# A feed-forward with ternary weights: four f32 passes become four f16 products with x1 split in two

## What is computed

```python
def _L0_ffn_ref(x, weight, bias):
    scale = jnp.mean(jnp.abs(weight))
    w_t = jnp.clip(jnp.round(weight / (scale + EPS)), -1.0, 1.0)
    w_ste = weight + jax.lax.stop_gradient(w_t * scale - weight)
    return jnp.einsum('bsi,oi->bso', x, w_ste) + bias
x = _layernorm(x + attn(x, ...))         # x1
x = _layernorm(x + _L0_ffn_ref(x, weight, bias))
```

## Time and profile before

| | us |
|---|---|
| median of 3 runs | 455.08 (454.64 to 455.99) |
| profiled execution | 455.08 |
| its span, first to last instruction | 453.1 |
| TensorE busy | 407.7 (90%) |
| VectorE busy | 351.8 (78%) |
| ScalarE busy | 277.0 (61%) |
| GpSimd busy | 227.7 (50%) |
| mean granted TensorE clock | 0.970 of 2.4 GHz |

### The profile page before, as it was taken

One profiled execution on the slowest core, in us unless ns is written; L12 is line 12 of the kernel. 1 busy time (PEld: TensorE's weight loads), 2 busy tenths in 40 slices (PEclk: granted clock), 3 DMA queues, 4 the chain that ended last, 5 costly groups with the idle time before them and its releaser, 6 DMA issues.

```text
span 453.1 us, 9004 instructions
## 1 busy us (share of the span) xinstructions
PE 407.7 (90%) x3361; PEld 350.7 (77%) x3363; DVE 351.8 (78%) x668; ACT 277.0 (61%) x802; POOL 227.7 (50%) x151
## 2 busy tenths in 40 slices
PE   6997888599898999999999999898989999998991
PEld 5996777479696878787879797787788888887880
DVE  3557897788898988889788878888798898972422
ACT  3556527857667675858484848584859595847200
POOL 2743120606456565656564636565546565654505
PEclk9999699889999999999999999999899999999997
DMA  8990007292242406040605060406050604060000
GB/s 257 259 341 9 1 0 210 94 255 53 44 59 48 93 14 94 14 93 13 95 13 93 13 92 16 93 13 95 12 94 13 94 14 93 14 94 13 0 13 23
DMA packets 80651, 33.43 MB, mean 74 GB/s; under 512 B 68960, under 2 KB 79200, under 8 KB 80352
## 3 DMA queue, kind: packets, MB, share of 16 engines
q1 hardware_dynamic: 79792, 32.53, 33.4%
q10 hardware_dynamic: 816, 0.33, 0.3%
HBM read 11.87 MB, written 4.19 MB: 35 GB/s over the span
## 4 chain that ended last, share of the span: by engine, by line
PE 59%; DVE 16%; issue 9%; ACT 9%; POOL 3%; DMA 2%; SPq 1%; POOLq 0%; ACTq 0%; DVEq 0%
PE PS L600 12%; PE PS L546 9%; PE PS L621 9%; PE PS L443 5%; ACT room_h L758 5%; PE PS L560 4%; DVE room_wg L1020 4%; PE PS L579 4%; PE PS L648 3%; PE PS L526 3%; PE PS L405 3%; DVE room_K L1035 2%; DVE aoT L1027 2%; PE PS L484 2%; PE PS L422 2%
## 5 line engine op out<-in xcount | busy, mean ns | idle before, releaser
L600 PE MATMUL PS<-Weff,aoT 128*128 128x256 f32 x768 | 97.1, 282 | 0.0
L600 PEld LDWEIGHTS PS<-Weff,aoT 128*128 128x128 f32 x768 | 91.6, 188 | 0.1
L1112 POOL TENSOR_TENSOR ny<-nx,nu 128x16 f32<-128x16 f32 x16 | 46.7, 2920 | 89.0 <-DVE nx L947 89.0
L1106 POOL TENSOR_TENSOR room_wg<-room_comp,keep 128x1024 f32<-128x1024 f32 x32 | 75.9, 2394 | 6.2 <-ACT room_comp L749 6.2
L621 PE MATMUL PS<-V,room_wg 128*128 128x129 f32 x512 | 67.8, 283 | 6.9 <-POOL room_wg L1106 2.5
L621 PEld LDWEIGHTS PS<-V,room_wg 128*128 128x128 f32 x512 | 63.4, 196 | 11.1 <-ACT room_h L758 4.0
L758 ACT ACTIVATE room_h<-PS,room_K 128x8 f32<-128x8 f32 (+7 forms) x256 | 70.4, 363 | 1.8 <-DVE room_K L974 1.7
L758 ACT ACTIVATION_READ_ACCUMULATOR room_h<-PS,room_K 128x1 f32 x256 | 62.0, 248 | 0.0
L672 ACT ACTIVATE room_wo<-PS 128x128 f32<-128x128 f32 (+7 forms) x16 | 10.4, 651 | 75.1 <-PE PS L639 75.1
L1027 DVE TENSOR_TENSOR aoT<-PS,aoT 128x1024 fp32r<-128x1024 f32 x32 | 38.9, 1224 | 16.8 <-ACT aoT L672 16.5
L546 PE MATMUL PS<-room_h,kT 128*128 128x512 f16 x192 | 46.5, 379 | 2.5 <-DVE aoT L1027 1.3
(11 more groups left out here) (151 smaller groups left out, 744.6 us busy)
## 6 DMA issues: line engine op xcount, KB each, us to landing
H<-in_L_attn_h SPq DMA_DIRECT2D x4, 512.0 KB, 6.3
room_wg<-in_L_attn_Wg SPq DMA_DIRECT2D x1, 2048.0 KB, 15.3
cw_rows<-room_wgT SPq DMA_DIRECT2D x1, 2048.0 KB, 6.8
CW<-cw_rows SPq DMA_DIRECT2D x1, 2048.0 KB, 8.1
out<-room_wo SPq DMA_DIRECT2D x16, 128.0 KB, 1.7
CW<-in_L_attn_Wq_up SPq DMA_DIRECT2D x2, 512.0 KB, 12.3
room_wo<-in_L_attn_Wo SPq DMA_DIRECT2D x1, 1024.0 KB, 17.7
room_h<-room_K SPq DMA_TRANSPOSE x64, 3.3
```

Source lines behind the costliest of these rows:

```text
L600: last = nc.tensor.matmul(o, aoT[:, ap, hd // 2, hd % 2, :, :].rearrange("p c q -> p (c q)"), Weff[:, wp, hd, :], start=mid and hd == n == ...
L1106: G.tensor_tensor(Pm[:, c, :, :], E[:, c, :, :], keep[:, :, :], ALU.mult).then_inc(g_mask, 1)
L1112: G.tensor_tensor(ny[:, 0:HEADS], nx[:, 0:HEADS], nu[:, 0:HEADS], ALU.pow).then_inc(g_rs, 1)
```

## The change

The ternary weights are kept without their scale, so that -1, 0 and 1 stand exactly in f16. x1 transposed is kept as two f16 values, a high part (ScalarE's copy) and a low part (what the copy left, subtracted by a new VectorE instruction out of PSUM, which signals `d_xl`). The feed-forward becomes four f16 products with one accumulation, high and low part for each of the two halves of the inner dimension, and waits for `d_xl` instead of ScalarE's `a_xt`. The scale is applied where z is made, which becomes a scalar_tensor_tensor, and z with its statistics moves behind the first rope products. In z's old place stands the new subtraction.

```diff
-        wfT = sb("wfT", [P, KC, HID])
+        wfT = sb("wfT", [P, 2, KC, HID], f16)[:, 0, :, :]
...
-        x1T = part(room_h, 2048, "p (k n) -> p k n", KC * P, k=KC)
+        x1T = part(room_h, 2048, "p (x k n) -> p x k n", KC * P, x=2, k=KC).bitcast(f16)
+        ternary = part(room_h, 3584, "p (k n) -> p k n", KC * HID, k=KC)
...
                 def feed_forward():
-                    pe.wait_ge(a_xt, i - 1)
+                    pe.wait_ge(d_xl, i - 1)
                     for k in range(KC):
-                        last = nc.tensor.matmul(ffn_bank(mid)[:, HID:2 * HID], x1T[:, k, :], wfT[:, k, :],
-                                                start=k == 0, stop=k == KC - 1)
+                        for n in range(2):
+                            last = nc.tensor.matmul(ffn_bank(mid)[:, HID:2 * HID], x1T[:, n, k, :], wfT[:, k, :],
+                                                    start=k == n == 0, stop=k == KC - 1 and n == 1)
...
-                    narrow(x1T[:, :, :], ffn_bank(mid)[:, HID:2 * HID].rearrange("p (k n) -> p k n", k=KC), a_xt)
+                    narrow(x1T[:, 0, :, :], ffn_bank(mid)[:, HID:2 * HID].rearrange("p (k n) -> p k n", k=KC), a_xt)
...
-            V_.tensor_scalar(fw_a[:, :, :], fw_s[:, :, :], fthr[:, 0:1], fscale[:, 0:1], ALU.is_gt, ALU.mult)
-            link(V_.tensor_scalar(fw_b[:, :, :], fw_s[:, :, :], fthn[:, 0:1], fscale[:, 0:1], ALU.is_lt, ALU.mult))
-            V_.tensor_tensor(wfT[:, :, :], fw_a[:, :, :], fw_b[:, :, :], ALU.subtract).then_inc(s_fw, 1)
+            V_.tensor_scalar(fw_a[:, :, :], fw_s[:, :, :], fthr[:, 0:1], 1.0, ALU.is_gt, ALU.mult)
+            link(V_.tensor_scalar(fw_b[:, :, :], fw_s[:, :, :], fthn[:, 0:1], 1.0, ALU.is_lt, ALU.mult))
+            V_.tensor_tensor(ternary[:, :, :], fw_a[:, :, :], fw_b[:, :, :], ALU.subtract).then_inc(s_fw, 1)
...
                 if ffn:
-                    dve.wait_ge(p_f, i - 1)
-                    dve.wait_ge(g_xb, i - 1)
-                    wait(dve, g_out, i - 2)
-                    V_.tensor_tensor(z[:, :], ffn_bank(mid)[:, HID:2 * HID], x1b, ALU.add).then_inc(d_fr, 1)
-                    dve.wait_ge(d_fr, i - 1)
-                    chained(V_.bn_stats(bns[:, 1, :], z[:, :]))
+                    dve.wait_ge(a_xt, i - 1)
+                    V_.tensor_tensor(x1T[:, 1, :, :], ffn_bank(mid)[:, HID:2 * HID].rearrange("p (k n) -> p k n", k=KC),
+                                     x1T[:, 0, :, :], ALU.subtract).then_inc(d_xl, 1)
...
                 if front:
                     rope_products(0)
+                if ffn:
+                    dve.wait_ge(p_f, i - 1)
+                    dve.wait_ge(g_xb, i - 1)
+                    wait(dve, g_out, i - 2)
+                    V_.scalar_tensor_tensor(z[:, :], ffn_bank(mid)[:, HID:2 * HID], fscale[:, 0:1], x1b, ALU.mult,
+                                            ALU.add).then_inc(d_fr, 1)
+                    dve.wait_ge(d_fr, i - 1)
+                    chained(V_.bn_stats(bns[:, 1, :], z[:, :]))
```

More of the change, by code:

```diff
@@ L192, in build @@
         d_nq, d_nl, g_rs = sem("d_nq"), sem("d_nl"), sem("g_rs")
-        d_red, d_qn, d_rope, d_add, d_cmax, d_rc, d_ql, d_ao, d_al, d_fr, d_y = (sem(n) for n in (
-            "d_red", "d_qn", "d_rope", "d_add", "d_cmax", "d_rc", "d_ql", "d_ao", "d_al", "d_fr", "d_y"))
+        d_red, d_qn, d_rope, d_add, d_cmax, d_rc, d_ql, d_ao, d_al, d_fr, d_y, d_xl = (sem(n) for n in (
+            "d_red", "d_qn", "d_rope", "d_add", "d_cmax", "d_rc", "d_ql", "d_ao", "d_al", "d_fr", "d_y", "d_xl"))
         g_mask, g_cn, g_rl, g_x1, g_xb, g_out = (sem(n) for n in ("g_mask", "g_cn", "g_rl", "g_x1", "g_xb", "g_out"))
@@ L494, in ffn_weights @@
                         last = nc.tensor.transpose(b[:, (2 * k + o) * P:(2 * k + o + 1) * P],
-                                                   wfT[:, o, k * P:(k + 1) * P], ident[:, :])
+                                                   ternary[:, o, k * P:(k + 1) * P], ident[:, :])
                 end(last)
```

## The result

| | before | changed |
|---|---|---|
| median, us | 454.94 (453.89 to 455.99, 6 runs) | 473.96 (470.45 to 475.62, 6 runs) |
| profiled execution, us | 455.08 | 470.84 |
| its span | 453.1 | 469.0 |
| mean granted clock | 0.970 | 0.976 |

The ratio is 1.0403, with a 95% interval of 1.0358 to 1.0449: slower by 4%.

A forecast was written before the change was run, and what follows sets the result against it. It took TensorE's chain to bound the kernel, with all engines meeting at the maximum over the block scores. To 455.08 us it added 16.4 for the wait, 0.5 for the end and 4.3 for the clock: 476.3, range 470.5 to 481.

The forecast's parts named there:

- the main term: TensorE's wait for VectorE's subtraction before the feed-forward, in 13 tiles: a loss of 16.4 us.
- (1): TensorE's feed-forward: four narrow f16 products take 0.43 us (bounds 0.43 to 0.86) instead of 1.01, gaining 0.58 per tile.
- (2): VectorE's new subtraction of 256 elements out of PSUM: 0.42 us, bounded by 0.3 and 0.6.
- (3): Feed-forward waits for the subtraction behind both reductions: 1.41 us in eight tiles, 0.99 to 1.08 in five, 16.4 in all.
- (4): z and statistics behind the first rope products: no cost, 0.85 if uncovered; z's new form 0 to 0.1 more, hidden.
- (5): The end: tile 15 gains 0.4 us, step 16 loses 1.0, step 17 gains 0.1; together a loss of 0.5.
- (7): TensorE's clock: eight new waits of 1.8 us bring three more falls to half clock, 4.3 us.
- A: TensorE's clock stays up: 472.0 us, or 470.7 with a handover 0.1 cheaper per tile; chance 0.22.
- steps 1 to 6: All parts of the change and the setup, without the clock: 16.9 us more, giving 472.0.
- B: Late TensorE catches up where VectorE bounds a tile's second half: 461 us; chance 0.06.
- C: Low part ready when TensorE reaches the products, so the kernel gets faster: 447 us; chance 0.02.
- D: Narrow products take 0.215 us each: 482, chance 0.05; or clock falls after nearly every long wait: 483, chance 0.08.

The follow-up runs named there:

- run 11: Run 6 with the projection's compressed blocks put before the feed-forward on TensorE in step 16: 445.81 us, ratio 0.9774.
- run 3: Changed kernel with all four products on the high part; VectorE's subtraction kept in place, reading another bank, but not waited for: 450.36 us, ratio 0.9895.
- run 5: Changed kernel with x1's path earlier on three queues: transposes before the queries, copy before the squares, subtraction before both reductions: 450.06 us, ratio 0.9895.
- run 1: Changed kernel with VectorE's subtraction moved between the two reductions of the squared queries: 458.15 us, ratio 1.0052.
- run 4: Kernel before the change with one wait added and no work: its f32 feed-forward also waits for VectorE's instruction behind both reductions: 474.63 us, ratio 1.0441.
- run 7: Changed kernel with the four products moved on TensorE from after window unit 1 to after unit 3: 457.11 us, ratio 1.0013.
- run 12: Changed kernel with the subtraction moved behind the first rope products too, which enlarges TensorE's stall: 497.23 us, ratio 1.0918.
- run 9: The changed kernel measured again as it is, to watch the clock: 474.96 us.
- run 6: Run 5 with z's statistics moved behind the maximum over the block scores: 451.09 us, ratio 0.9887.
- run 8: Changed kernel with the subtraction between the reductions, the products after window unit 3 and z's statistics behind the maximum: 451.39 us, ratio 0.9904.

## Why the prediction was right, and where it was not

The time, 473.96, lies in the range of 470.5 to 481.0, the sign and the size of the main term are right, and the forecast of 476.3 was 2.3 us too high. By its steps:

(1) The narrow products: 0.43 plus 0.17 for the restart made 0.60; the chain shows 0.61, and 0.44 without a wait (run 11). Right, and the upper bound of 0.215 each is out.

(2) The subtraction: 0.42, measured 0.42. As a duration right; as a cost in a queue it is 0.26 to 0.29 (runs 3 and 5). In the sum the duration was the right one to take, since TensorE waited for its end.

(3) The wait. In tile i = 5 the products end 1.17 us after VectorE's scaling starts (190.33 to 191.50), as the prediction had it. The periods of the tiles grew by 1.39 to 1.45 in nine tiles and by 0.97 to 1.08 in four, so 16.8 in all against 16.4. The prediction had eight and five, and so have the expectations of runs 1, 4, 7 and 12: it counted i = 11 among the short ones. That tile stood behind the one fall of the clock, which had made its queries late; the same step of the other batch (i = 3) belongs to the long ones, and without a fall i = 11 paid 1.40 as well. That one tile is the difference of 0.4.

(4) z is covered: it started without a wait in all tiles with a front. Its new form takes 476 ns where L953 took 424, 0.05 more; the prediction's bounds were 0 and 0.1. The maximum's idle time grew by 1.06 in i = 5 (0.42 to 1.48) and not by 1.3, since VectorE's own added work brings it there 0.36 later (4.91 us from its first reduction, 4.55 before).

(5) The end: 0.7 instead of 0.5. Step 15 gained 0.43, as said. Step 16 lost 0.8 instead of 1.0. Step 17 lost 0.2 where I had a gain of 0.1: between the projection's last sum and z 6.26 us pass instead of 6.05. The products gave 0.50 back and the subtraction with its handover took 0.46, near enough as said. The loss lies before them: the clock had already fallen when x1's transposes began (the fall at 460.17, they at 460.77), and they held up the copy by 0.25 more than in the kernel before, where it fell behind them (at 446.66, they at 445.17).

(7) **The step that failed is the clock.** It put three more falls behind the eight new waits, 4.3 us, by counting waits of 1.8 us or more as one class in one trace of the kernel before. In the two traces of the changed kernel there are 15 new waits of 1.80 to 1.82 us (nine in the first, six in the second, where waits behind a fall are shorter), and no fall behind any. The falls in the tiles stand behind the old wait for the outputs' transposes, of 1.87 to 1.88 us as in the earlier trace rows. The prediction's five long waits were in fact one of 1.80, three of 1.88 and one of 1.98, and the two falls came behind the 1.98 and a 1.88. Whether the length matters or the kind of work around the wait was not separated: waits of 1.80 us before the same transposes had no fall either, in 14 of 14 traces, so length is not ruled out; yet of the waits of 1.87 to 1.88 only 15 in 42 had one, so length alone does not decide.

What step 7 left out is the one new wait that did bring falls, that of 2.50 us in step 16: in three of eight traces, for 1.7 us each, so about 0.6 us on the average.

The totals give the term's size. Without the one fall in its tiles the kernel before is 17.2 us faster by the two profiled executions, and the medians are 19.0 apart. The changed kernel spent 29.6 us at half clock on the average of 12 runs and the kernel before 25.2 (33 runs of the series); at 1.3 us for a fall of 3.4 us, an estimate from run 9, that makes 1.7 of these 1.8. So the term was 1.7 us and not 4.3. The range could not show that: the 472.0 without the term lies in it too. Whether more of it than the 0.6 belongs to the change, or chance gave it, stays open.

The rule of the Trainium skill ("TensorE: Matmul & The Clock Gate", section "HAM oscillation — how this bites in real kernels") that I had set against this term came out closer for the new waits in the tiles: those of 1.80 to 1.82 us did nothing. For the old ones the trace goes on contradicting it, and so do the wait of 2.50 us in step 16 (run 9) and run 12 for waits of 2.6 to 3.0 us.

The rivals: A (the clock stays up, 472.0) describes the first trace, 470.84, in which the sum of steps 1 to 6 was 16.9 and the measured 15.8 (17.2 without the fall that only the kernel before had). B (slack eats the stall) is out by the periods: each tile paid in full. C (faster) is what runs 5, 6 and 8 made by moving the work, to 450 to 451 and not 447. D is out with the price of the products, and its second half with the clock, which fell behind none of the new waits in the tiles.

## What to carry to other kernels

Before you move an operand's last step to another engine, look up where that engine is in its queue at that moment: here 0.42 us of work, on an engine with a fifth of its time free, cost 16 us over 13 tiles, as it stood behind 1.3 us of reductions that the waiting engine had never had to wait for. The remedy was order and not speed: the same instructions, with x1's path ahead of the queries' path on three queues, the statistics behind the maximum and the projection's blocks ahead at the end, turned 1.040 into 0.977. What the late statistics and the new end would give the kernel before was not run, so 0.977 is not the gain of the narrow products by themselves. After each such move, look again for who is late next; at first it was TensorE, then VectorE before the maximum.

## What the runs showed of the hardware

- A restart of TensorE behind a wait costs more than the pitch: 0.17 us with f16 weights, in the products (0.61 against 0.44 in run 11) as in the window scores (0.82 against 0.65).
- The same kernel's executions differ by 3.4 us stretches at 1.2 GHz, each worth 0.9 to 1.4 us in the tiles and 1.7 in step 16; two traces of the changed kernel, 470.84 and 477.65, differ by 6.8 us, of which 4.0 lie in the tiles, 1.1 before them and 1.7 behind. To compare two variants that differ by 2 us, the stretch of the tiles without its falls told more than the median of four runs (runs 5 and 6, and 11).
- In 14 traces none of TensorE's 92 waits of 1.2 to 1.82 us had a fall of the clock behind it, 15 of 42 of 1.87 to 1.88 us had one, and so had all 14 of 3.6 us.
- VectorE's subtraction of 256 columns lasts 0.41 us, and the next instruction starts 0.33 us after it does (run 5).
